# A linear recurrence taken two steps at a time, in SBUF, with the PSUM banks freed at the product

## The chip, the cores and the metric

The kernel runs on one core of one Trainium2 chip. The metric is the device time of one execution in microseconds (us).

## The reference, cut to what matters

A block of three layers on x (4 batches of 256 rows, 256 wide): cross-attention over 4,096 keys, a linear recurrence, and a mixture of experts. The change lies in the recurrence. For each batch and head it keeps a state of 16 ranks by 16 dimensions:

```python
def step(M, inp):
    q_t, k_t, v_t, g_t = inp
    M = M * decay + jnp.einsum('bhr,bhd->bhrd', g_t * k_t * scale, v_t)
    y = jnp.einsum('bhr,bhrd->bhd', q_t, M)
    return (M, y)
xs = (q_r.transpose(1, 0, 2, 3), k_r.transpose(1, 0, 2, 3), v.transpose(1, 0, 2, 3), g.transpose(1, 0, 2, 3))
M0 = jnp.zeros((b, h, r, d), dtype=x.dtype)
_, Y = jax.lax.scan(step, M0, xs)
```

Its output goes through a linear layer and a layer norm; then come a router that picks two of eight experts per row, the experts, and a shared feed-forward layer.

## The kernel before

Five engines run programs written out by hand and meet at semaphores: TensorE (PE), VectorE (DVE), ScalarE (ACT), GpSimd (POOL) and SyncE (SP), which issues the DMAs. Attention takes most of the time: 32 pairs of heads, each in 16 chunks. For each half chunk ACT makes the exponentials `PR`, and POOL adds them up in `acc` (L1803), for the row sums; after the last one it folds `acc` into `accf` (L1811).

The recurrence turns time into columns. A tile of 128 partitions holds 8 heads with 16 ranks each; the 512 columns are two batches of 256 time steps. With two halves of the heads and two pairs of batches there are four groups n, and in each 16 dimensions of the value, so 64 steps J = 16 n + s (`STEPS` is 16), each a whole recurrence over time for one dimension. A step is

- PE (L585, L586): the broadcast. Two matmuls spread one dimension of the value (`vh` and `vl`) over the ranks, into PSUM bank 4 or 5, by the parity of J.
- DVE (L1390): the product with the gated keys `kk`, in place in that bank.
- DVE (L1394): the scan over time, state = `dect` x state + product, out of `dect` (SBUF) and the bank (PSUM) into `M` (SBUF), which has two places.
- POOL (L1742): `qm` = `M` x queries `qr`, all in SBUF; eight places.
- PE (`sum_r`, L597): for every four steps the sum over ranks of four `qm`, issued within step 4q + 6, between that step's broadcast and the next.

`dect` is the decay, zero where a batch begins (from `seq`). The waits around a step: PE's broadcast of step J waits for the scan of step J - 2 (`m_done`), since the bank is free only then; DVE's product waits for the broadcast (`vb_ps`); the scan waits for the `qm` of step J - 2 (`qm_ready`), and POOL for the scan.

The order of the work around it is fixed by the program text. Steps 0 to 11 lie within the last three chunks of attention, two behind each half chunk; there POOL's `qm` stand between its sums of `acc`. Then come the last pair of heads' row sums, `copy_l`, `invert_l` and `divide`, the output projection and `add_rows` (L1320), with steps 12 to 15 between; the layer norm `norm_stats` and `norm_apply` (L1358); PE's transposes; and steps 18 to 47 with the projections of groups 2 and 3 between them (`lin_q`, `lin_k`, `lin_gate`, `lin_v`, `ranks` on PE, `rotate`, `keys`, `values_lo` on DVE), POOL's bias additions with steps 20 to 35 (L1749, L1751), and in group 2 the first half's output projection `mix_out` (L608), `add_out` (L1400), two more layer norms, `scale_rows` (L1405), the router (`below_max`, L1427, and `best_two`, from L1432) and the shared layer (`shared_product`, L1458). Steps 48 to 63 stand between the layers of the first experts (L653).

Of the kernel before, what the change touches and what calls it, by code (L numbers as in the profile page):

```python
# [27 lines left out]
def program(nc, nb, top, d, out):  # L28
# [4 lines left out]
    with ctx:  # L33
# [10 lines left out]
        def room(*tensors):  # L44
# [33 lines left out]
        we, = room(("we", [P, 3, 6, DM], F32))  # L78
        wel, gw, iota, sw12, sw3, be, hT, hTs, wT0, yacc0, t3, bc, zs, zT, lg, cand, sc2, hot, mx, sm, wm, wmT, *st_bc = room(
            ("wel", [P, 3, 6, DM], F32R), ("gw", [P, 2, E], F32), ("iota", [P, E], F32), ("sw12", [P, 2, 2, W], F32), ("sw3", [P, 4, DM], F32),  # L80
            ("be", [P, E, 3, 2], F32), ("hT", [P, 2, 2, W], F32), ("hTs", [P, 2, 2, W], F32R), ("wT0", [P, 2, W], F32),
            ("yacc0", [P, 2, W], F32), ("t3", [P, 2, 2, W], F32), ("bc", [P, 2, 2, W], F32), ("zs", [P, 2, W], F32), ("zT", [P, 4, W], F32),
            *[(x, [P, HR, E], F32) for x in ("lg", "cand", "sc2", "hot")], ("mx", [P, HR], F32), ("sm", [P, HR], F32),
            ("wm", [P, HR, 2 * E], F32), ("wmT", [2 * E, 2, W], F32), *norm_tiles("b"), *norm_tiles("c"))
        st_b, st_c = st_bc[0:3], st_bc[3:6]
# [159 lines left out]
        def _(sp):  # L245
# [190 lines left out]
        def _(pe):  # L436
# [139 lines left out]
            def step(J):  # L576
                n, s = J // STEPS, J % STEPS
                g, dd = n % 2, 4 * (s % 4) + s // 4
                if s == 0:
                    pe.wait_ge(vlo, n + 1)  # L580
                if J >= 2:
                    pe.wait_ge(m_done, J - 1)
                else:
                    pe.wait_ge([qr_ready, kk_ready][J], 2)
                pe.matmul(ps[:, 4 + J % 2, :], selvr[:, dd, :], vh[:, g, :], start=True, stop=False)  # L585
                pe.matmul(ps[:, 4 + J % 2, :], selvr[:, dd, :], vl[:, g, :], start=False, stop=True).then_inc(vb_ps, 1)  # L586
                if J >= 6 and J % 4 == 2:
# [671 lines left out]
        def _(dve):  # L1259
# [474 lines left out]
        def _(pool):  # L1734
            def step(J):
# [191 lines left out]
```

## Time and profile before

| | us |
|---|---|
| median of 3 runs | 2115.67 |
| lowest and highest run | 2111.74, 2115.80 |
| the profiled execution | 2115.32 |
| its span, first to last instruction | 2113.5 |
| PE busy in the span | 2016.6 (95%) |
| DVE busy | 1550.5 (73%) |
| POOL busy | 1434.4 (68%) |
| ACT busy | 1236.7 (59%) |

Busy shares are means over stages with different limits. The recurrence runs from 1757 to 1968 us of the span; what a change to it does is read from the rows of that stretch. Times in rows count from the span's start.

### The profile page before, as it was taken

The numbers are of one execution on the slowest core, as the hardware profiler recorded it, in microseconds if no ns is written. First come the engines' busy times: TensorE is split into PE (matmuls) and PEld (weight loads), VectorE is DVE, ScalarE is ACT, GpSimd is POOL, SyncE is SP. The second block draws the span as 40 slices with busy tenths as digits, with TensorE's granted clock in tenths as the row PEclk, the third lists the DMA queues.
The fourth block names the chain that finished last, engine by engine and source line by source line (L and its number), as shares of the span: only waits on it lengthen the run. The fifth ranks groups of instructions, "written<-read, shape, count | busy, mean of one in ns | idle before, by whom it ended". The sixth has DMA issues, their size and how long they took to land.

```text
span 2113.5 us, 47661 instructions
## 1 busy us (share of the span) xinstructions
PE 2016.6 (95%) x19694; PEld 1491.0 (71%) x19694; DVE 1550.5 (73%) x2004; ACT 1236.7 (59%) x1590; POOL 1434.4 (68%) x685
## 2 busy tenths in 40 slices
PE   5899999999999999999999999999999997779998
PEld 4677777777777777777777777777777743335466
DVE  5677777877777778777777787777777736887757
ACT  4566766676666676767666766676666662111333
POOL 3477777777777777777777777777777756633227
PEclk8999999999999999999999999999999998889999
DMA  8110101210101013101000130101010110203222
GB/s 219 29 27 14 29 14 34 74 29 14 29 14 29 15 33 75 28 18 25 23 20 25 23 87 16 29 14 29 14 29 4 47 39 1 76 29 97 76 60 71
DMA packets 45764, 82.15 MB, mean 39 GB/s; under 512 B 7120, under 2 KB 29008, under 8 KB 44912
## 3 DMA queue, kind: packets, MB, share of 16 engines
q1 hardware_dynamic: 45552, 79.10, 13.8%
q8 instruction: 160, 2.62, 0.5%
q14 instruction: 52, 0.43, 0.1%
HBM read 74.03 MB, written 5.05 MB: 37 GB/s over the span
## 4 chain that ended last, share of the span: by engine, by line
PE 79%; DVE 12%; issue 4%; POOL 2%; ACT 1%; DMA 1%; SPq 1%; POOLq 0%; DVEq 0%; ACTq 0%
PE ps L503 19%; PE ps L495 16%; PE ps L469 12%; PE ps L458 10%; PE ps L487 7%; PE ps L653 6%; DVE amx L1285 5%; DVE Otn L1307 2%; PE ps L449 1%; DVE V L1270 1%; PE ps L518 1%; DVE KL L1266 1%; PE ps L633 1%; POOL qm L1742 1%; PE ps L540 1%
## 5 line engine op out<-in xcount | busy, mean ns | idle before, releaser
L1803 POOL TENSOR_TENSOR acc<-acc,PR 128x1024 f32<-128x1024 f32 x480 | 1150.5, 2397 | 348.8 <-ACT PR L1156 310.1
L1285 DVE TENSOR_REDUCE amx<-ps 128x2 f32<-128x1024 f32 x512 | 623.9, 1219 | 195.9 <-PE ps L487 190.2
L1156 ACT ACTIVATE PR<-ps 128x1024 f32<-128x1024 f32 x512 | 518.8, 1019 | 208.9 <-PE ps L495 195.1
L503 PE MATMUL ps<-PR,V 128*64 128x256 f32 x4096 | 499.4, 386 | 0.4 <-ACT PR L1156 0.3
L503 PEld LDWEIGHTS ps<-PR,V 128*64 128x64 f32 x4096 | 271.2, 136 | 164.4 <-issue 27.2
L1006 ACT ACTIVATE ps<-NM 128x1024 f32<-128x1024 f32 x231 | 236.6, 1026 | 203.0 <-DVE V L1270 176.5
L469 PE MATMUL ps<-wv,C 64*128 64x256 f32 x4608 | 315.7, 281 | 1.2
L469 PEld LDWEIGHTS ps<-wv,C 64*128 64x128 f32 x4608 | 305.5, 187 | 11.9 <-issue 4.3
L458 PE MATMUL ps<-C,wk 64*128 64x512 f32 x2304 | 308.7, 395 | 5.3 <-DVE C L1262 4.2
L495 PE MATMUL ps<-qh,KH 64*128 64x256 f32 x2048 | 311.0, 297 | 0.8 <-ACT ps L1006 0.7
L495 PE MATMUL ps<-ql,KH 64*128 64x256 f32 x2048 | 293.4, 280 | 0.0
L495 PE MATMUL ps<-qh,KL 64*128 64x256 f32 x2048 | 293.1, 279 | 0.0
L495 PEld LDWEIGHTS ps<-qh,KH 64*128 64x128 f32 x2048 | 199.1, 186 | 76.1 <-issue 68.2
L458 PEld LDWEIGHTS ps<-C,wk 64*128 64x128 f32 x2304 | 221.5, 187 | 40.5 <-issue 8.6
L487 PE MATMUL ps<-KH,qh 64*128 64x512 f32 x1024 | 226.2, 437 | 23.0 <-DVE amx L1285 13.4
L1266 DVE TENSOR_TENSOR KL<-ps,KH 128x512 fp32r<-128x512 f32 x256 | 164.6, 685 | 61.9 <-ACT KH L997 59.5
L1567 DVE COPY ps<-NM 128x512 f32<-128x512 f32 x217 | 149.7, 690 | 76.1 <-ACT PR L1156 72.7
L495 PEld LDWEIGHTS ps<-ql,KH 64*128 64x128 f32 x2048 | 198.2, 187 | 5.6
L495 PEld LDWEIGHTS ps<-qh,KL 64*128 64x128 f32 x2048 | 198.1, 187 | 0.0
L997 ACT ACTIVATE KH<-ps 128x512 fp32r<-128x512 f32 x256 | 138.5, 593 | 90.0 <-PE ps L458 90.0
L1270 DVE COPY V<-ps 128x512 f32<-128x512 f32 x248 | 158.9, 682 | 19.7 <-PE ps L469 19.7
L487 PEld LDWEIGHTS ps<-KH,qh 64*128 64x128 f32 x1024 | 97.2, 186 | 92.0 <-issue 42.5
(198 smaller groups left out, 1900.2 us busy)
## 6 DMA issues: line engine op xcount, KB each, us to landing
wk<-wk_split SPq DMA_DIRECT2D x62, 192.0 KB, 3.4
wv<-wv_split SPq DMA_DIRECT2D x30, 384.0 KB, 4.8
bc<-wm_rows SPq DMA_DIRECT2D x32, 256.0 KB, 4.2
craw<-in_ctx SPq DMA_DIRECT2D x30, 256.0 KB, 4.2
we<-in_we SPq DMA_DIRECT2D x10, 768.0 KB, 4.4
wq<-in_wq SPq DMA_DIRECT2D x32, 128.0 KB, 2.9
wo<-in_wo SPq DMA_DIRECT2D x64, 64.0 KB, 2.2
craw<-in_ctx SPq DMA_DIRECT2D x30, 128.0 KB, 4.1
```

The lines of the kernel that those rows point to most:

```text
L458: mm = pe.matmul(out, wk[half(h), slot, 3 * w + t, :], C[half(h), 3 * c + t, j * CH:j * CH + CH], start=(i == 0), stop=(i == len(PARTS) - 1))
L469: mm = pe.matmul(out[:, k * 256:k * 256 + 256], C[half(h), 3 * c + t, keys], wv[half(h), 3 * w + t, :], start=(i == 0 and k == 0), stop=(i ...
L487: mm = pe.matmul(ps[:, 4 + h, :], qh[half(h), slot, t * P:t * P + P], KH[slot][half(h), c, :], start=True, stop=True)
L495: mm = pe.matmul(ps[:, first_bank + h, k * ROWS:k * ROWS + ROWS], keys_of[slot][half(h), c, keys], q[half(h), slot, :], start=False, stop= ...
L503: mm = pe.matmul(psO[half(h), :], V[:, c * KT + 2 * hf + k, hd * DH:hd * DH + DH], PR[:, slot, h, k, :], start=(first and hf == 0 and k == ...
L1006: act.activation(ps[:, first_bank:first_bank + 2, :].rearrange("p h (k n) -> p h k n", k=2), row.unsqueeze(2).to_broadcast([P, 2, 2, ROWS] ...
L1156: act.activation(PR[:, pr_slot(t, hf), :, :, :].rearrange("p h k n -> p (h k n)"), ps[:, bank:bank + 2, :].rearrange("p h n -> p (h n)"), ...
L1266: dve.tensor_tensor(KL[slot][:, c, :], bank, KH[slot][:, c, :].bitcast(F32), ALU.subtract).then_inc(k_lo, 1)
L1270: dve.tensor_copy(V[:, k:k + 2, :].rearrange("p a n -> p (a n)"), bank).then_inc(v_sb, 1)
L1285: dve.tensor_reduce(amx[:, :, t, c], psG, AX.X, ALU.max).then_inc(g_max, 1)
L1567: dve.tensor_copy(ps[:, score_bank(t, 1) + 1, :].rearrange("p (k n) -> p k n", k=2), NM[:, 1:2, :].to_broadcast([P, 2, ROWS])).then_inc(se ...
L1803: pool.tensor_tensor(flat(acc[:, :, :, :]), flat(acc[:, :, :, :]), flat(PR[:, pr_slot(t, hf), :, :, :]), ALU.add).then_inc(acc_done, 1)
```

## The change

Steps 0 to 47 are taken in pairs (J, J + 1). PE and POOL keep their instructions in their order. On DVE a pair is one product over both banks, 1,024 columns, that writes into two places of `M`, and one scan over the same 1,024 columns that reads `dect` and `M` and writes `M` in place. `M` has four places instead of two and `dect` holds every decay twice, side by side, so that one scan runs through two steps (the zero at the beginning of a batch cuts the state). Steps 48 to 63 have the same two instructions with 512 columns each. PE's broadcast waits for `kv_ready`, which the product raises, and no longer for `m_done` of the scan. The product waits for the `qm` of the pair before last. To make room, `seq` is loaded into the fourth place of `M`, and `ow` gets a place and a load later, behind `add_rows` of the last pair of heads.

```diff
-            ("t2", [P, 2, W], F32), ("gate", [P, W], F32), ("uT", [P, 2, 2, W], F32), ("dect", [P, 2, W], F32),
+            ("t2", [P, 2, W], F32), ("gate", [P, W], F32), ("uT", [P, 2, 2, W], F32), ("dect", [P, 2, 2, W], F32),
...
-            ("M", [P, 2, W], F32), ("qm", [P, 8, W], F32), ("selvr", [P, 16, P], F32R),
+            ("M", [P, 4, W], F32), ("qm", [P, 8, W], F32), ("selvr", [P, 16, P], F32R),
...
-        yT = uT
+        yT, seq = uT, M[:, 3, :]
...
-                sp.dma_start(ow[:], d["ow"]).then_inc(ow_in, 16)
...
             sp.wait_ge(x_added, PAIRS)
+            sp.dma_start(ow[:], d["ow"]).then_inc(ow_in, 16)
...
                 if J >= 2:
-                    pe.wait_ge(m_done, J - 1)
+                    pe.wait_ge(kv_ready, J - 1)
...
-            def step(J):
+            def steps(J, k):
+
                 n, s = J // STEPS, J % STEPS
-                g = n % 2
                 if s == 0:
                     dve.wait_ge(kk_ready, n + 1)
-                dve.wait_ge(vb_ps, J + 1)
-
-                bank = ps[:, 4 + J % 2, :]
-                dve.tensor_tensor(bank, bank, kk[:, g, :], ALU.mult).then_inc(kv_ready, 1)
-                dve.wait_ge(kv_ready, J + 1)
-                if J >= 2:
-                    dve.wait_ge(qm_ready, J - 1)
-                dve.tensor_tensor_scan(M[:, J % 2, :], dect[:, g, :], bank, 0.0, ALU.mult, ALU.add).then_inc(m_done, 1)
+                dve.wait_ge(vb_ps, J + k)
+                if J >= 4:
+                    dve.wait_ge(qm_ready, J + k - 4)
+                state = M[:, J % 4:J % 4 + k, :].rearrange("p a n -> p (a n)")
+                decay = dect[:, n % 2, 0:k, :].rearrange("p a n -> p (a n)")
+                dve.tensor_tensor(M[:, J % 4:J % 4 + k, :], ps[:, 4 + J % 2:4 + J % 2 + k, :],
+                                  kk[:, n % 2:n % 2 + 1, :].to_broadcast([P, k, W]), ALU.mult).then_inc(kv_ready, k)
+                dve.wait_ge(kv_ready, J + k)
+                dve.tensor_tensor_scan(state, decay, state, 0.0, ALU.mult, ALU.add).then_inc(m_done, k)
...
-                    for k in range(2 * EARLY):
-                        step(2 * EARLY * (t - 13) + k)
+                    for k in range(0, 2 * EARLY, 2):
+                        steps(2 * EARLY * (t - 13) + k, 2)
...
-            for J in range(6 * EARLY + 4, STEPS + 1):
-                step(J)
+            steps(STEPS, 2)
             norm_apply(na, 1, row, st_a)
             for n in range(3):
                 for s in range(STEPS):
-                    if STEPS * n + s <= STEPS:
+                    if STEPS * n + s <= STEPS + 1:
                         continue
-                    step(STEPS * n + s)
+                    if s % 2 == 0:
+                        steps(STEPS * n + s, 2)
```

On DVE, from the end of attention to the division of the last pair of heads; a row is line, operation, what it writes and reads, partitions by columns, and the semaphores it waits for (the scan is printed as SCALAR_TENSOR_TENSOR). Before:

```order
L1390 TENSOR_TENSOR ps<-ps,kk 128x512 [waits vb_ps]
L1394 SCALAR_TENSOR_TENSOR M<-dect,ps 128x512 [waits qm_ready,kv_ready]
L1299 COPY Ou<-ps 128x256 [waits ot_ready,pv_done]
L1320 TENSOR_TENSOR x<-ps,x 128x512 [waits x_added,out_ps]
L1390 TENSOR_TENSOR ps<-ps,kk 128x512 [waits vb_ps]
L1394 SCALAR_TENSOR_TENSOR M<-dect,ps 128x512 [waits qm_ready,kv_ready]
L1390 TENSOR_TENSOR ps<-ps,kk 128x512 [waits vb_ps]
L1394 SCALAR_TENSOR_TENSOR M<-dect,ps 128x512 [waits qm_ready,kv_ready]
L1303 COPY Otn<-ps 128x256 [waits l_ps]
L1307 RECIPROCAL Otn<-Otn 128x256 [waits l_sb]
L1313 TENSOR_TENSOR Otn<-Ou,Otn 128x256 [waits o_sb,rl_ready]
```

With the change:

```order
L1392 TENSOR_TENSOR M<-ps,kk 128x1024 [waits qm_ready,vb_ps]
L1395 SCALAR_TENSOR_TENSOR M<-dect,M 128x1024 [waits kv_ready]
L1299 COPY Ou<-ps 128x256 [waits ot_ready,pv_done]
L1320 TENSOR_TENSOR x<-ps,x 128x512 [waits x_added,out_ps]
L1392 TENSOR_TENSOR M<-ps,kk 128x1024 [waits qm_ready,vb_ps]
L1395 SCALAR_TENSOR_TENSOR M<-dect,M 128x1024 [waits kv_ready]
L1303 COPY Otn<-ps 128x256 [waits l_ps]
L1307 RECIPROCAL Otn<-Otn 128x256 [waits l_sb]
L1313 TENSOR_TENSOR Otn<-Ou,Otn 128x256 [waits o_sb,rl_ready]
L1392 TENSOR_TENSOR M<-ps,kk 128x1024 [waits qm_ready,vb_ps]
L1395 SCALAR_TENSOR_TENSOR M<-dect,M 128x1024 [waits kv_ready]
```

Two rows take the place of four, the product writes `M` and waits for `qm_ready`, the scan reads `M` in place of `ps` and waits for nothing but the product, and only one pair stands ahead of `copy_l`.

On DVE, ahead of the router's maximum (L1427, with the change L1428) in group 2. Before, with step 44 ahead of it and step 45 behind:

```order
L1390 TENSOR_TENSOR ps<-ps,kk 128x512 [waits vb_ps]
L1394 SCALAR_TENSOR_TENSOR M<-dect,ps 128x512 [waits qm_ready,kv_ready]
L1427 TENSOR_REDUCE mx<-ps 128x4 [waits lg_ps,g_in]
L1428 TENSOR_TENSOR lg<-ps,mx 128x32 [waits chain]
L1390 TENSOR_TENSOR ps<-ps,kk 128x512 [waits vb_ps,chain]
L1394 SCALAR_TENSOR_TENSOR M<-dect,ps 128x512 [waits qm_ready,kv_ready]
L1432 TENSOR_REDUCE sm<-lg 128x4 [waits ex]
```

With the change:

```order
L1392 TENSOR_TENSOR M<-ps,kk 128x1024 [waits qm_ready,vb_ps]
L1395 SCALAR_TENSOR_TENSOR M<-dect,M 128x1024 [waits kv_ready]
L1392 TENSOR_TENSOR M<-ps,kk 128x1024 [waits qm_ready,vb_ps]
L1395 SCALAR_TENSOR_TENSOR M<-dect,M 128x1024 [waits kv_ready]
L1428 TENSOR_REDUCE mx<-ps 128x4 [waits lg_ps,g_in]
L1429 TENSOR_TENSOR lg<-ps,mx 128x32 [waits chain]
L1433 TENSOR_REDUCE sm<-lg 128x4 [waits ex,chain]
```

Step 45 has moved ahead of the maximum, into the pair with step 44. In the same way step 17 has moved ahead of `norm_apply`, step 37 ahead of `add_out`, step 39 ahead of the `norm_apply` before the router and step 47 ahead of the shared products.

## Rows read from the trace of the kernel before

**Rows 1.** The page, its part on the chain that ended last: shares by engine.

```profile
PE 79%; DVE 12%; issue 4%; POOL 2%; ACT 1%; DMA 1%; SPq 1%; POOLq 0%; DVEq 0%; ACTq 0%
```

**Rows 2.** Busy time by stretch: length, each engine busy, PEclk, DMA share, GB/s.

```profile
1757.30:1785.40 28.10, 20.19 (x112) 10.38 (x112) 23.63 (x28) 6.33 (x6) 25.37 (x17) 0.88 0.00 1
1785.40:1804.70 19.30, 11.14 (x32) 5.12 (x33) 17.68 (x29) 1.52 (x5) 8.75 (x7) 0.52 0.35 118
1804.70:1854.90 50.20, 42.84 (x136) 19.83 (x136) 41.24 (x50) 6.22 (x8) 34.92 (x35) 0.88 0.08 34
1854.90:1907.30 52.40, 39.40 (x145) 20.08 (x145) 47.16 (x89) 9.06 (x17) 19.96 (x16) 0.87 0.15 51
1907.30:1968.00 60.70, 60.70 (x179) 28.85 (x177) 45.85 (x62) 6.79 (x10) 24.04 (x20) 1.00 0.30 87
```

**Rows 3.** Waits, 1757 to 1907 us: total, times, longest.

```profile
DVE ps L1390 <- PE ps L586: 12.9, 15, 2.7
```

**Rows 4.** Groups of DVE, shapes apart: count, busy us, mean ns, idle before.

```profile
L1285 DVE TENSOR_REDUCE amx<-ps 128x2 f32<-128x1024 f32 x512 | 623.9, 1219 | 195.9 <-PE ps L487 190.2
...
L1394 DVE TENSOR_TENSOR_SCAN M<-dect,ps 128x512 f32<-128x512 f32 x64 | 78.1, 1221 | 6.9 <-POOL qm L1742 4.8
...
L1390 DVE TENSOR_TENSOR ps<-ps,kk 128x512 f32<-128x512 f32 x64 | 44.1, 689 | 21.0 <-PE ps L586 20.9
...
L1703 DVE TENSOR_TENSOR wTs<-wT,wTs 128x1024 fp32r<-128x1024 f32 x1 | 1.2, 1215 | 0.0
```

**Rows 5.** Timeline of DVE, steps 20, 23, 26 and 35: start, duration.

```profile
1811.83 0.70 DVE L1390 TENSOR_TENSOR ps<-ps,kk 128x512 f32<-128x512 f32 x1 [0.90 <-PE ps L586]
...
1820.10 0.69 DVE L1390 TENSOR_TENSOR ps<-ps,kk 128x512 f32<-128x512 f32 x1
...
1825.65 0.68 DVE L1390 TENSOR_TENSOR ps<-ps,kk 128x512 f32<-128x512 f32 x1
...
1847.89 1.22 DVE L1394 TENSOR_TENSOR_SCAN M<-dect,ps 128x512 f32<-128x512 f32 x1
```

**Rows 6.** Timeline of POOL: `qm`, two `qm`, the fold of `acc`, a bias.

```profile
1759.44 1.27 POOL L1742 TENSOR_TENSOR qm<-M,qr 128x512 f32<-128x512 f32 x1 [10.78 <-DVE M L1394]
...
1764.79 2.50 POOL L1742 TENSOR_TENSOR qm<-M,qr 128x512 f32<-128x512 f32 x2
...
1784.08 1.27 POOL L1811 TENSOR_TENSOR accf<-acc 128x512 f32<-128x512 f32 x1
...
1825.28 0.73 POOL L1749 TENSOR_TENSOR u<-u,vecs 128x256 f32<-128x256 f32 x1
```

**Rows 7.** Timelines of DVE and POOL where both have two SBUF inputs.

```profile
391.23 2.37 POOL L1803 TENSOR_TENSOR acc<-acc,PR 128x1024 f32<-128x1024 f32 x1
392.50 2.71 DVE L1262 TENSOR_TENSOR C<-craw,C 128x1536 fp32r<-128x1536 f32 x1
393.74 3.72 POOL L1803 TENSOR_TENSOR acc<-acc,PR 128x1024 f32<-128x1024 f32 x1
...
1860.02 1.53 DVE L1405 SCALAR_TENSOR_TENSOR u<-u,mvb,vecs 128x256 f32<-128x256 f32 x1
...
2059.41 1.75 DVE L1498 TENSOR_TENSOR lox<-rawx,hix 128x1536 fp32r<-128x1536 f32 x1
2059.51 2.80 POOL L1766 TENSOR_TENSOR hTs<-hT,hTs 128x512 fp32r<-128x512 f32 x1 [2.58 <-ACT hTs L1066]
```

**Rows 8.** Timeline of PE: the sum over ranks at two clocks.

```profile
1805.85 1.94 PE L597 MATMUL ps<-qm,sely 128*32 128x512 f32 x8
...
1824.95 1.07 PE L597 MATMUL ps<-qm,sely 128*32 128x512 f32 x8
```

**Rows 9.** The second matmul of the broadcast: shortest, median and longest ns.

```profile
L586 PE MATMUL ps<-vl,selvr x64: 387/397/632, 1751.5 to 1964.2; 128*128 128x512 f32 x64
```

**Rows 10.** Timeline of DVE: step 45's product and the start of `best_two`.

```profile
1886.01 0.70 DVE L1390 TENSOR_TENSOR ps<-ps,kk 128x512 f32<-128x512 f32 x1 [1.71 <-PE ps L586]
...
1887.88 0.16 DVE L1432 TENSOR_REDUCE sm<-lg 128x4 f32<-128x32 f32 x1
```

More of the change, by code:

```diff
@@ L54, in program @@
         norm_tiles = lambda x: [("st6" + x, [P, NR, 6], F32), ("mv" + x, [P, NR, 2], F32), ("rs" + x, [P, NR], F32)]
-        (w4, bd, rope, t1, t2, gate, uT, dect, qr, kk, vh, vl, M, qm, selvr, ow, vecs, u, seq, sely, dl, dec, gb, *st_a) = room(
+        (w4, bd, rope, t1, t2, gate, uT, dect, qr, kk, vh, vl, M, qm, selvr, vecs, u, sely, dl, dec, gb, *st_a) = room(
             ("w4", [P, 4, 2, DM], F32), ("bd", [P, 2, 2, 2, P], F32), ("rope", [P, 2, W], F32), ("t1", [P, 2, W], F32),
-            ("t2", [P, 2, W], F32), ("gate", [P, W], F32), ("uT", [P, 2, 2, W], F32), ("dect", [P, 2, W], F32),
+            ("t2", [P, 2, W], F32), ("gate", [P, W], F32), ("uT", [P, 2, 2, W], F32), ("dect", [P, 2, 2, W], F32),
             ("qr", [P, 2, W], F32), ("kk", [P, 2, W], F32), ("vh", [P, 2, W], F32R), ("vl", [P, 2, W], F32R),
-            ("M", [P, 2, W], F32), ("qm", [P, 8, W], F32), ("selvr", [P, 16, P], F32R),
-            ("ow", [P, 2, DM], F32), ("vecs", [P, 3, DM], F32), ("u", [P, NR, DM], F32), ("seq", [P, W], F32),
+            ("M", [P, 4, W], F32), ("qm", [P, 8, W], F32), ("selvr", [P, 16, P], F32R),
+            ("vecs", [P, 3, DM], F32), ("u", [P, NR, DM], F32),
             ("sely", [P, 4, 32], F32), ("dl", [P, 2], F32), ("dec", [P, 2], F32), ("gb", [P, 2], F32), *norm_tiles("a"))
-        yT = uT
+        yT, seq = uT, M[:, 3, :]
         selv = qm[:, 0:4, :].rearrange("p a n -> p (a n)").rearrange("p (e c) -> p e c", e=16)
@@ L78, in program @@
         we, = room(("we", [P, 3, 6, DM], F32))
[L79 removed]
+        wel, gw, iota, sw12, sw3, be, hT, hTs, wT0, yacc0, t3, bc, zs, zT, lg, cand, sc2, hot, mx, sm, wm, wmT, ow, *st_bc = room(
             ("wel", [P, 3, 6, DM], F32R), ("gw", [P, 2, E], F32), ("iota", [P, E], F32), ("sw12", [P, 2, 2, W], F32), ("sw3", [P, 4, DM], F32),
@@ L83, in program @@
             *[(x, [P, HR, E], F32) for x in ("lg", "cand", "sc2", "hot")], ("mx", [P, HR], F32), ("sm", [P, HR], F32),
-            ("wm", [P, HR, 2 * E], F32), ("wmT", [2 * E, 2, W], F32), *norm_tiles("b"), *norm_tiles("c"))
+            ("wm", [P, HR, 2 * E], F32), ("wmT", [2 * E, 2, W], F32), ("ow", [P, 2, DM], F32), *norm_tiles("b"), *norm_tiles("c"))
         st_b, st_c = st_bc[0:3], st_bc[3:6]
@@ L328, in load_early @@
                 sp.dma_start(dl[:], d["dl"]).then_inc(r_in, 16)
-                sp.dma_start(seq[:], d["seq"][:, 0:W]).then_inc(r_in, 16)
+                sp.dma_start(seq, d["seq"][:, 0:W]).then_inc(r_in, 16)
                 sp.dma_start(bd[:], d["bd"]).then_inc(r_in, 16)
@@ L1515, in early @@
                     for g in range(2):
-                        dve.tensor_scalar(dect[:, g, :], seq[:, :], dec[:, g:g + 1], None, ALU.mult).then_inc(dect_ready, 1)
+                        dve.tensor_scalar(dect[:, g, :, :], seq.unsqueeze(1).to_broadcast([P, 2, W]), dec[:, g:g + 1], None, ALU.mult).then_inc(dect_ready, 1)
                     keys(0)
@@ L1620, in _ @@
             add_rows(nb - 1, PAIRS - 2, ps[:, 2, :])
-            step(6 * EARLY)
-            step(6 * EARLY + 1)
+            steps(6 * EARLY, 2)
             copy_l(PAIRS)
@@ L1625, in _ @@
             divide(PAIRS)
-            step(6 * EARLY + 2)
-            step(6 * EARLY + 3)
+            steps(6 * EARLY + 2, 2)
             add_rows(nb - 1, PAIRS - 1, ps[:, 0, :])
@@ L1666, in _ @@
             for s in range(4):
-                step(3 * STEPS + s)
+                steps(3 * STEPS + s, 1)
                 if s in (0, 1):
@@ L1673, in _ @@
                 weigh_third(X)
-                step(3 * STEPS + 4 + 3 * X)
+                steps(3 * STEPS + 4 + 3 * X, 1)
                 if X == 0:
@@ L1677, in _ @@
                 mask_third(X)
-                step(3 * STEPS + 5 + 3 * X)
+                steps(3 * STEPS + 5 + 3 * X, 1)
                 weigh_first(X + 1)
-                step(3 * STEPS + 6 + 3 * X)
+                steps(3 * STEPS + 6 + 3 * X, 1)
                 second_by_third(X)
@@ L1741, in step @@
                     pool.wait_ge(y_ps, J // 4 - 1)
-                pool.tensor_tensor(qm[:, J % 8, :], M[:, J % 2, :], qr[:, n % 2, :], ALU.mult).then_inc(qm_ready, 1)
+                pool.tensor_tensor(qm[:, J % 8, :], M[:, J % 4, :], qr[:, n % 2, :], ALU.mult).then_inc(qm_ready, 1)
             def biases(i):
```

## The prediction, on record before the changed kernel ran

> **What bounds the kernel now.** I read five views in turn. The chain of waits first: TensorE (PE) holds 79% of it, but PE's share is an average over the whole program [rows 1], and the change touches only the recurrence. So, second, the busy time by stretch [rows 2]. I cut the recurrence into A (end of attention), B (to the first broadcast behind the transposes), C (to `add_out`), D (to the first expert layer) and E (experts). PE fills E, 60.70 of 60.70 us. In A it is GpSimd (POOL) with 25.37 of 28.10 us, in B to D VectorE (DVE) is the busiest with 17.68 of 19.30, 41.24 of 50.20 and 47.16 of 52.40. A to D add up to 150 us, and what they lose moves everything behind them. Third, who waits for whom: DVE waits 12.9 us, in 15 places, for a broadcast [rows 3]. Fourth, what a step costs: product 689 ns, scan 1221 ns [rows 4]; undisturbed, three steps take 1825.65 - 1820.10 = 5.55 us, 1.85 each [rows 5]. Fifth, what DVE and POOL do to each other [rows 7], on which the sum turns.
>
> **The price of a pair on DVE.** The 1,024-column product reads PSUM as the chunk maximum does, 1219 ns for 1,024 columns; a subtraction from SBUF to SBUF takes 1215 [rows 4]: 1.22. The scan: a 512-column product and one of 1,536 (689 and 1750 ns [rows 4, 7]) give about 1.04 ns per column and 0.15 us fixed; the scan's 1221 ns is then 2 x 512 x 1.04 and the same fixed part, so 1,024 columns take 2.29. Back to back a step runs 0.06 us under its two durations, a pair then 3.45: 0.25 less than two steps, 6 us over 24 pairs. The bounds of a scan are 2.13 (no fixed part) and 2.44 (two scans); I take 2.29. The Trainium skill ("VectorE: DVE Perf Modes", the TRN2 errata) gives an operation out of SBUF 62 cycles less of fixed cost than one out of PSUM; by it, an estimate, 24 scans would save 1.6 us more. The two 1,024-column rows, 1215 and 1219 ns, show no such difference, and I take none.
>
> **The scan's second input.** Before, the scan read `dect` from SBUF and `ps` from PSUM; now both inputs are in SBUF. What such an operation does beside POOL is in [rows 7]. DVE's 1,536-column subtraction starts at 2059.41 and ends at 2061.16; POOL's product started at 2059.51 takes 2.80 instead of 1.27 [rows 6] and ends 1.15 after it: it stood still. The other way round, POOL's sum ran from 391.23 to 393.60; DVE's subtraction, begun at 392.50, took 2.71 instead of 1.75 and ended 1.61 after that sum; the next sum (393.74) then took 3.72. So one stands until the other is done, and a waiting one gets in between two of the other engine's. The scan of before overlaps `qm` without loss, having one input in SBUF. No row shows a scan with two. Bounds: nothing, or the full standstill; I take the full one, since three operations with two SBUF inputs (a product on POOL, a subtraction on DVE, and the 256 columns at 1860.02, which took 1.53, more than 1,024 columns elsewhere) all show it. The Trainium skill ("SBUF — State Buffer", Who interferes with whom) words this for every DVE instruction with two SBUF inputs beside a POOL instruction that reads SBUF: by it the sum is the one below, without it that of the first rival; for the scan no row of before decides.
>
> A scan that gets in between two POOL operations then lengthens POOL's chain by 2.29 - 0.15 + 1.15 - 1.24 = 2.05 us (1.24 is the spacing of two `qm` [rows 6]).
>
> **A.** POOL works without a gap to speak of from 1759.44 to `accf`'s end, 1784.08 + 1.27 = 1785.35 [rows 6]. Six scans (steps 2 to 13) now fall into this chain, the sixth before `accf` because DVE may run two pairs ahead: 6 x 2.05 = 12.3. The first `qm` starts 1.6 later (3.51 for a pair instead of 1.91), and 0.5 of idle time takes some of it. A: +13.4.
>
> **B.** `copy_l` used to wait behind steps 12 and 13 (-3.5). The division stands for one `qm` (+0.5); the pair 14, 15 must wait for step 15's broadcast, behind a row sum (+1.6); the pair 16, 17 stands whole ahead of `norm_apply` (+1.6), which now meets two `qm` instead of one (+1.05). B: +1.2.
>
> **C.** The first pair needs steps 18 and 19, with a row sum (1.94 us behind stretch B, whose granted clock of 0.52 is near the lower level of 1.2 GHz, 1.07 at the upper [rows 2, 8]) between them: +2.5. Then steps 20 to 35, where POOL has a `qm` (1.24) and a bias (0.7) per step. From the end of a scan, T: the product ends at T+1.2; the first `qm` (started T+0.14) lets go just then, the scan gets in and ends at T+3.5; the bias, then the second `qm`, end at T+4.0 and T+5.3. PE's row sum waits for that `qm`, and the pair's second broadcast stands behind it, two matmuls of 0.40 [rows 9]: T+6.3, T+6.9. Product to T+8.1; the scan finds the next pair's second `qm` running, waits to T+9.15 and ends at T+11.3. Four steps take 11.3 us instead of (1847.89 + 1.22 - 1811.83)/4 = 9.3 [rows 5]: +7.9 over sixteen. At the end `add_out` waits for steps 36 and 37: +1.3. C: +11.7.
>
> **D.** Step 37 no longer stands between the statistics and `scale_rows` (-1.85, -1.05 for the standstill at 1860.02, +0.35 for the root it hid); the pair 38, 39 stands ahead of `norm_apply` (+1.6, and +1.0 for a second `qm`); two steps as a pair (-0.25). `below_max` now waits for the pair 44, 45, whose second broadcast came at 1886.0: 1886.0 + 3.5, 0.9 for maximum and exponential, so `best_two` starts at 1890.4 by the old clock instead of 1887.88 [rows 10]: +2.5. The whole pair 46, 47 stands ahead of the shared products: +1.5. D: +3.8.
>
> **E and the small edits.** Steps 48 to 63 stay single; their scans too now have two SBUF inputs, but DVE has 15 us to spare against PE there [rows 2]: nothing. `dect`, twice as wide, is made before the recurrence, with DVE then idle for `vh`. `ow` loads from `add_rows` on, at the end of B; POOL's step 20 waits for it, several steps later, and SP's queue is one load longer, 70 us before the shared products need what follows. All at nothing.
>
> **Sum.** 13.4 + 1.2 + 11.7 + 3.8 = 30.1 us on the profiled execution's 2115.3 (span 2113.5; the median of the runs is 2115.67, 0.4 above): 2145.4, I say 2145.
>
> **The rivals.**
> *No standstill* (the scan does not share a path with POOL). Then A costs +1.1 (the first `qm`), B +0.6, C +2.8 (the paired broadcasts, less 0.25 a pair), D +3.8: +8.3, 2124. For it: no row has a scan with two SBUF inputs. Against: every other such operation stood. 12%.
> *Faster:* banks free at the product. A broadcast may start 2.3 us earlier, so that the 12.9 us for which DVE waits [rows 3] vanish, with 0.25 for each of the 18 pairs outside A: -17, 2098. It decides only if there is no standstill and both broadcasts of a pair, with the row sum or projection between them, end within a scan's 2.29 us. For it: between 1820.10 and 1825.65 DVE waits for no broadcast at all [rows 5]. Against: one row sum at the lower clock alone takes 1.94. 5%.
> *The change doesn't do what it says*, pairs being held by other waits so that gains and losses cancel: 2115. 3%.
> *More than I say:* POOL goes first each time (four steps in 12.4: +4.4) and PE runs at 1.2 GHz through C (row sum and broadcast 1.5 longer [rows 8, 9], four times: +6): 2156, the upper end of my own case.
>
> **How the numbers follow.** My case has 80%; its own range is 2130 to 2156. 2122 to 2156 takes in half of the first rival too and leaves out no more than 2 in 10. A change of 0.2%, 4 us, is about what a measurement of this kernel can tell from none. Slower: my case and the first rival, less what falls near zero: 0.90; same 0.05; faster 0.05.
>
> **What would show it.** The scan's row: 2.29 us where POOL is idle, and 3 us and more for many in A and C; `qm` with a maximum of about 3.5 us, never over 1.3 before. `accf` ends some 13 us later, `add_out` some 26, the first expert layer some 30; E keeps its 60.7. If scans stay at 2.29 and `qm` at 1.27 everywhere, the standstill was wrong; if A's POOL chain is no longer than before, the sum is.

## The result and the profile after

| | us |
|---|---|
| before, median of 4 runs beside those of the change | 2115.74 (2111.74 to 2118.18) |
| after, median of 4 runs | 2146.59 (2142.77 to 2149.57) |
| ratio, 95% interval | 1.0145, 1.0133 to 1.0157 |
| profiled execution of after; its span | 2146.78; 2145.0 |

The change costs 31 us, and all but 0.2 of it lies in A to D. Cut at the same events as before, the busy time by stretch of the kernel after (columns as in [rows 2]: length, PE, PEld, DVE, ACT, POOL, PEclk, DMA share, GB/s):

```profile
1757.30:1798.80 41.50, 24.07 (x112) 12.40 (x112) 28.06 (x17) 6.33 (x6) 37.10 (x17) 0.74 0.00 0
1798.80:1819.40 20.60, 9.65 (x33) 4.54 (x33) 15.56 (x22) 1.52 (x5) 10.11 (x9) 0.67 0.49 168
1819.40:1880.90 61.50, 47.47 (x148) 21.62 (x149) 43.51 (x30) 6.22 (x8) 43.26 (x34) 0.82 0.03 13
1880.90:1938.70 57.80, 37.25 (x134) 19.73 (x133) 44.65 (x77) 8.95 (x17) 19.72 (x16) 0.85 0.15 46
1938.70:1999.40 60.70, 60.70 (x181) 28.88 (x183) 47.30 (x62) 6.79 (x10) 24.09 (x20) 1.00 0.31 87
```

The reader should hold two columns of this against [rows 2]. E is 60.70 us again, with PE full. In A and C it is POOL that has more to do, 37.10 instead of 25.37 and 43.26 instead of 34.92 us, with the same number of instructions in A: some of them take longer. The groups of the kernel after, shapes apart (count, busy us and mean ns, idle before), say which:

```profile
L1395 DVE TENSOR_TENSOR_SCAN M<-dect,M 128x1024 f32<-128x1024 f32 x24 | 60.0, 2500 | 2.5
L1392 DVE TENSOR_TENSOR M<-ps,kk 128x1024 f32<-128x1024 f32 x24 | 29.3, 1220 | 39.9 <-PE ps L586 20.3 <-issue 13.5 <-POOL qm L1741 6.0
...
L1741 POOL TENSOR_TENSOR qm<-M,qr 128x512 f32<-128x512 f32 x64 | 90.8, 1430 | 115.9 <-DVE M L1395 106.2 <-issue 9.7
```

The paired product is what was forecast, 1.22 us. The paired scan has a mean of 2.50 where 2.29 was the price alone, and DVE idles 39.9 us ahead of the 24 products, 20.3 of them put down to a broadcast. The timeline of POOL in stretch A of the kernel after shows the mechanism:

```profile
1761.62 4.47 POOL L1741 TENSOR_TENSOR qm<-M,qr 128x512 f32<-128x512 f32 x2 [12.45 <-DVE M L1395]
1766.05 2.34 POOL L1802 TENSOR_TENSOR acc<-acc,PR 128x1024 f32<-128x1024 f32 x1
1768.35 4.49 POOL L1741 TENSOR_TENSOR qm<-M,qr 128x512 f32<-128x512 f32 x2
...
1775.13 2.54 POOL L1741 TENSOR_TENSOR qm<-M,qr 128x512 f32<-128x512 f32 x2
1777.62 4.34 POOL L1802 TENSOR_TENSOR acc<-acc,PR 128x1024 f32<-128x1024 f32 x1
1781.91 4.48 POOL L1741 TENSOR_TENSOR qm<-M,qr 128x512 f32<-128x512 f32 x2
...
1791.11 4.34 POOL L1802 TENSOR_TENSOR acc<-acc,PR 128x1024 f32<-128x1024 f32 x1
1795.53 3.27 POOL L1810 TENSOR_TENSOR accf<-acc 128x512 f32<-128x512 f32 x1
```

Two `qm` take 2.50 us [rows 6] and here 4.47, 4.49 and 4.48 in three cases; the sum into `acc` takes 2.37 [rows 7] and here 4.34 twice; `accf` 3.27 instead of 1.27. That is six times 1.97 to 2.00 us, 11.9 in all, where POOL stands while a scan gets in. In C three biases and two `qm` stand, and at other times the scans themselves; the timelines of DVE and POOL of the kernel after, around steps 22 to 25:

```profile
1834.21 1.23 DVE L1392 TENSOR_TENSOR M<-ps,kk 128x1024 f32<-128x1024 f32 x1 [0.69 <-issue]
1835.54 2.29 DVE L1395 TENSOR_TENSOR_SCAN M<-dect,M 128x1024 f32<-128x1024 f32 x1
...
1840.24 3.42 DVE L1395 TENSOR_TENSOR_SCAN M<-dect,M 128x1024 f32<-128x1024 f32 x1
```

```profile
1835.55 2.81 POOL L1750 TENSOR_TENSOR x<-x,vecs 128x256 f32<-128x256 f32 x1
...
1840.22 1.29 POOL L1741 TENSOR_TENSOR qm<-M,qr 128x512 f32<-128x512 f32 x1
1841.45 2.73 POOL L1750 TENSOR_TENSOR x<-x,vecs 128x256 f32<-128x256 f32 x1
```

A bias that starts 0.01 us after a scan takes 2.81 instead of 0.73 [rows 6]; a scan that starts 0.02 us after a `qm` takes 3.42 instead of 2.29. In both cases whoever came second stood.

### The profile page after: what moved, and what is told of

It is laid out like the page before. It is cut to its first block and busy times, and to the rows that moved or that the text cites. A ratio compares the mean times of both kernels' runs of the same rounds, so it can differ in the third digit from the quotient of the medians.

```text
span 2145.0 us, 47615 instructions
## 1 busy us (share of the span) xinstructions
PE 2021.8 (94%) x19694; PEld 1493.4 (70%) x19694; DVE 1554.1 (72%) x1956; ACT 1236.5 (58%) x1590; POOL 1455.8 (68%) x685
## 5 line engine op out<-in xcount | busy, mean ns | idle before, releaser
L469 PEld LDWEIGHTS ps<-wv,C 64*128 64x128 f32 x4608 | 305.5, 187 | 11.9 <-issue 4.3
L458 PEld LDWEIGHTS ps<-C,wk 64*128 64x128 f32 x2304 | 220.7, 187 | 40.9 <-issue 8.5
L1741 POOL TENSOR_TENSOR qm<-M,qr 128x512 f32<-128x512 f32 x64 | 90.8, 1430 | 115.9 <-DVE M L1395 106.2
```

The lines of the kernel that those rows point to most:

```text
L458: mm = pe.matmul(out, wk[half(h), slot, 3 * w + t, :], C[half(h), 3 * c + t, j * CH:j * CH + CH], start=(i == 0), stop=(i == len(PARTS) - 1))
L469: mm = pe.matmul(out[:, k * 256:k * 256 + 256], C[half(h), 3 * c + t, keys], wv[half(h), 3 * w + t, :], start=(i == 0 and k == 0), stop=(i ...
```

## The experiments

Eight kernels ran, each beside the kernel before on the same chip. For each one the stretches of its profiled execution were cut at the events of [rows 2]; A is counted from the start of `vl`'s step (1756.75 before), so that what the attention ahead of it varies by is left out. "16 steps" is from the product of step 20 to the end of the scan of step 35, a part of C. The table gives the lengths in us.

| kernel | median | ratio, 95% interval | A | B | C | 16 steps | D |
|---|---|---|---|---|---|---|---|
| before | | | 28.6 | 19.4 | 50.2 | 37.3 | 52.4 |
| after | 2146.59 | 1.0133 to 1.0157 | 41.5 | 20.6 | 61.5 | 44.5 | 57.8 |
| e1, POOL only writes in B to D | 2141.33 | 1.0108 to 1.0142 | 41.5 | 20.5 | 57.7 | 40.9 | 56.9 |
| e2, single steps into SBUF | 2130.88 | 1.006 to 1.0091 | 39.1 | 18.2 | 55.9 | 45.3 | 53.6 |
| e3, pairs out of the banks | 2162.97 | 1.0215 to 1.0246 | 34.9 | 23.9 | 76.7 | 58.1 | 61.6 |
| e4, only four places in `M` | 2113.47 | 0.998 to 0.9998 | 28.6 | 16.4 | 49.8 | 37.2 | 52.4 |
| e5, third group single | 2138.86 | 1.0102 to 1.0133 | 41.4 | 20.5 | 58.9 | 44.9 | 53.6 |
| e6, A single, out of the banks | 2134.15 | 1.008 to 1.011 | 28.6 | 19.0 | 62.3 | 44.5 | 59.8 |
| e7, PE's order in pairs too | 2142.32 | 1.0117 to 1.0145 | 41.4 | 20.4 | 59.7 | 42.0 | 54.3 |
| e8, e7 and POOL only writes | 2122.16 | 1.0021 to 1.0052 | 34.2 | 20.4 | 48.3 | 31.8 | 53.4 |

Before ran at a median of 2114.15 beside e1, e2, e3 and e6, at 2114.78 beside e4, e5 and e7, at 2116.72 beside e8.

The theory at the start: the scan of after has two SBUF inputs and excludes POOL's operations with two SBUF inputs (the *standstill*), and a pair waits for its second broadcast. The rivals: the standstill is not what costs, or pairing by itself costs nothing. In e1 and e8 POOL leaves out products and biases and only writes in their place, so these two measure time and nothing else.

**e1: POOL's reads taken away in B, C and D.**

```
-                pool.tensor_tensor(qm[:, J % 8, :], M[:, J % 4, :], qr[:, n % 2, :], ALU.mult).then_inc(qm_ready, 1)
+                if STEPS <= J < 3 * STEPS:
+                    pool.wait_ge(qm_ready, J)
+                    pool.memset(t3[:, :, :, :].rearrange("p a m n -> p (a m n)")[:, 0:1360], 0.0).then_inc(qm_ready, 1)
+                    return
+                pool.tensor_tensor(qm[:, J % 8, :], M[:, J % 4, :], qr[:, n % 2, :], ALU.mult).then_inc(qm_ready, 1)
```

The two biases became memsets of 688 columns in the same way.

> The changed kernel with POOL's qm of steps 16 to 47 and its biases replaced by memsets of about the same length (1,360 and 688 columns), which write SBUF and read nothing; the sums over ranks then add up old values and the biases are left out. Theory (a scan with two SBUF inputs and a POOL operation that reads SBUF stand still for one another): scans in stretches C and D take 2.29 to 2.35 us each, none above 2.5, the memsets keep their own length, steps 20 to 35 take 37 to 39 us instead of 44.5, and the time is 2135 to 2141. Rival (the cost is that of pairs: two broadcasts awaited, whole pairs ahead of the work behind): the time stays within 2 us of 2146.6. Stretch A is unchanged under both, its fold of acc ending 13 us later than in the kernel before.

Measured: 2141.33, just outside. The groups of e1 for the scan and the product (shapes apart, columns as above):

```profile
L1395 DVE TENSOR_TENSOR_SCAN M<-dect,M 128x1024 f32<-128x1024 f32 x24 | 57.3, 2387 | 2.5
L1392 DVE TENSOR_TENSOR M<-ps,kk 128x1024 f32<-128x1024 f32 x24 | 29.3, 1220 | 38.8 <-PE ps L586 22.2 <-issue 15.4 <-POOL qm L1745 1.2
```

The mean of the scan still holds the scans of A, up to 3.07 us. In C every scan takes 2.29 and every memset of 1,360 columns 1.23 us, also where the one starts 0.03 us behind the other; from the timeline of e1:

```profile
1851.07 2.29 DVE L1395 TENSOR_TENSOR_SCAN M<-dect,M 128x1024 f32<-128x1024 f32 x1
1851.10 1.23 POOL L1743 MEMSET t<- 128x1360 f32 x1
```

The standstill is gone there. But the 16 steps fall from 44.5 to 40.9 only, not to 37 to 39; the idle time ahead of the products stays at 38.8 us. So the standstill is real and its removal alone is worth little in C: DVE then waits for the broadcasts, and the 16 steps stay 3.6 us above before.

**e2: single steps in the old order, the product into SBUF.** The pairs go, the second SBUF input stays.

```
-                    for k in range(0, 2 * EARLY, 2):
-                        steps(2 * EARLY * (t - 13) + k, 2)
+                    for k in range(2 * EARLY):
+                        steps(2 * EARLY * (t - 13) + k, 1)
...
-                    if s % 2 == 0:
-                        steps(STEPS * n + s, 2)
+                    steps(STEPS * n + s, 1)
```

> Single steps in the order of the kernel before, but each product written into M and scanned there, with banks free at the product and four places in M. Theory (standstill): scans of 512 columns range from 1.22 to above 2.2 us, qm up to 2.4 us; twelve scans of 1.22 in stretch A's POOL chain cost 12 x (1.22 - 0.15 + 1.15 - 1.24) = 11.8 us, so that the fold of acc ends 11 to 13 us later than before; the time is 2130 to 2138. Rival (pairs): nothing of it is left, 2112 to 2117.

Measured: 2130.88, as the theory has it. A stays 10.5 us above before and C 5.7, while B is 1.1 below it and D 1.1 above. In the 16 steps single steps lose 8.0 us, more than the 7.2 of the pairs. Two rows of POOL in stretch A of e2, a sum and a double `qm`, show that single scans, too, let POOL stand:

```profile
1764.01 3.26 POOL L1804 TENSOR_TENSOR acc<-acc,PR 128x1024 f32<-128x1024 f32 x1
1767.24 4.35 POOL L1743 TENSOR_TENSOR qm<-M,qr 128x512 f32<-128x512 f32 x2
```

**e3: pairs, product and scan in the banks.** The second SBUF input goes, the pairs stay; the banks come free at the scan's end, as before the change.

```
-                    pe.wait_ge(kv_ready, J - 1)
+                    pe.wait_ge(m_done, J - 1)
...
-                state = M[:, J % 4:J % 4 + k, :].rearrange("p a n -> p (a n)")
-                dve.tensor_tensor(M[:, J % 4:J % 4 + k, :], ps[:, 4 + J % 2:4 + J % 2 + k, :],
-                                  kk[:, n % 2:n % 2 + 1, :].to_broadcast([P, k, W]), ALU.mult).then_inc(kv_ready, k)
+                bank = ps[:, 4 + J % 2:4 + J % 2 + k, :]
+                dve.tensor_tensor(bank, bank, kk[:, n % 2:n % 2 + 1, :].to_broadcast([P, k, W]), ALU.mult).then_inc(kv_ready, k)
...
-                dve.tensor_tensor_scan(state, decay, state, 0.0, ALU.mult, ALU.add).then_inc(m_done, k)
+                dve.tensor_tensor_scan(state, decay, bank.rearrange("p a n -> p (a n)"), 0.0, ALU.mult, ALU.add).then_inc(m_done, k)
```

> Pairs as in the change, but the product stays in its two banks and the scan of 1,024 columns reads them, so that the scan has one SBUF input and banks are free at its end. Theory (standstill): every scan takes 2.29 us and every qm at most 1.30; the fold of acc ends at most 4 us later than before. The time does not come back to that of before, since both broadcasts of a pair now follow the last scan: 2122 to 2140. Rival (pairs alone): 2145 or more, and the fold of acc as late as in the changed kernel, 13 us.

Measured: 2162.97, a clear miss, slower than after itself. What the theory said of the standstill holds: the scan's mean is 2287 ns and that of `qm` 1275, its longest 1.32 us. But A is 6.3 us longer than before, where at most 4 was expected. What the theory left out shows in the groups and in DVE's waits from 1757 to 1960 us of e3 (engine, awaited, total, times, longest):

```profile
L1395 DVE TENSOR_TENSOR_SCAN M<-dect,ps 128x1024 f32<-128x1024 f32 x24 | 54.9, 2287 | 2.2
L1741 POOL TENSOR_TENSOR qm<-M,qr 128x512 f32<-128x512 f32 x64 | 81.0, 1275 | 153.1 <-DVE M L1395 141.1 <-issue 12.0
...
DVE ps L1391 <- PE ps L586: 65.7, 21, 7.3
```

and in one pair's round, all engines of e3 in order of time:

```profile
1830.64 2.29 DVE L1395 TENSOR_TENSOR_SCAN M<-dect,ps 128x1024 f32<-128x1024 f32 x1
...
1832.98 0.50 PE L585 MATMUL ps<-vh,selvr 128*128 128x512 f32 x1 [3.77 <-DVE M L1395]
...
1833.72 1.94 PE L597 MATMUL ps<-qm,sely 128*32 128x512 f32 x8
...
1838.28 0.40 PE L586 MATMUL ps<-vl,selvr 128*128 128x512 f32 x1
1838.78 1.23 DVE L1391 TENSOR_TENSOR ps<-ps,kk 128x1024 f32<-128x1024 f32 x1 [4.68 <-PE ps L586]
```

Both banks are held until the scan ends (1832.93); only then does PE write the first, sum the rows, multiply a projection and write the second. In this round PE does nothing while DVE scans, and the pair takes 9.5 us (7.3 is the mean over the 16 steps). Neither e1 nor e3 has the standstill in C; they differ there above all in when the banks come free, and the 16 steps take 40.9 and 58.1 us. So it is the early release that makes pairs bearable.

**e6: after, with the 16 steps of A single and out of the banks.** In A the body of `steps` does as before; the broadcasts there wait for `m_done`.

```
+                if J < STEPS:
+                    for j in range(J, J + k):
+                        bank = ps[:, 4 + j % 2, :]
+                        dve.tensor_tensor(bank, bank, kk[:, n % 2, :], ALU.mult).then_inc(kv_ready, 1)
...
+                        dve.tensor_tensor_scan(M[:, j % 4, :], dect[:, n % 2, 0, :], bank, 0.0, ALU.mult, ALU.add).then_inc(m_done, 1)
+                    return
```

> The changed kernel with steps 0 to 15 single and scanned out of PSUM, as before; pairs in SBUF from step 16 on. Theory (standstill): stretch A loses nothing but a place or two in the order, the fold of acc ends within 2 us of the kernel before, and the time is 2131 to 2136. Rival (in A only the later first qm of a pair counts, 1.6 us): 2144 to 2146.

Measured: 2134.15. A is 28.6 us, that of before to 0.1, and the time falls by 12.4: what A loses is lost to the whole kernel. D is 2.1 us longer than in after. 2.0 of these lie behind the start of `best_two`, where the granted clock is 0.93 instead of 1.00 and DVE waits 3.59 us instead of 2.11 for the broadcast of step 48; why the clock was lower there is open. As e6 takes the pairs out of A too, it does not by itself tell them from the second input; e2, which has single steps with that input, does.

**e4: of the change only the four places of `M`.** The wider `dect` and the later load of `ow` stay as well. Single steps, product and scan in the bank, banks released at the scan's end; the scan waits for the row product of four steps back and not of two. Against the kernel before:

```
-                if J >= 2:
-                    dve.wait_ge(qm_ready, J - 1)
-                dve.tensor_tensor_scan(M[:, J % 2, :], dect[:, g, :], bank, 0.0, ALU.mult, ALU.add).then_inc(m_done, 1)
+                if J >= 4:
+                    dve.wait_ge(qm_ready, J + k - 4)
+                dve.tensor_tensor_scan(state, decay, bank.rearrange("p a n -> p (a n)"), 0.0, ALU.mult, ALU.add).then_inc(m_done, k)
```

> Single steps with product and scan out of the bank, as before; of the change only four places in M are kept. Theory (the product into SBUF, and with it the scan's second SBUF input, is what costs single steps 15 us): the wait of a scan for the row product two steps back goes, POOL sets A as before (accf ends within 0.5 us of before), the copy of the sums in B need not stand behind steps 12 and 13 (-3), and C and D do not move, since DVE waits there for broadcasts that still start at the end of a scan: 2112, between 2109 and 2115. Scans 1.22 and row products 1.27 us throughout. Rival (the places themselves, the wider decay, the moved load or the order cost something): above 2118.

Measured: 2113.47, ratio 0.9989 (0.998 to 0.9998): a gain at the edge of what can be told, and none of the rival's cost. B is 3.0 us shorter. A row of DVE in B of the kernel before, the scan of step 12, and the same scan in e4:

```profile
1786.68 1.22 DVE L1394 TENSOR_TENSOR_SCAN M<-dect,ps 128x512 f32<-128x512 f32 x1 [1.52 <-POOL qm L1742]
```

```profile
1784.61 1.22 DVE L1395 TENSOR_TENSOR_SCAN M<-dect,ps 128x512 f32<-128x512 f32 x1
```

The 1.52 us for `qm` are gone. e2 and e4 have the same steps in the same order; they differ in where the product goes and when the bank comes free, and in 17 us. The bank comes free earlier in e2, the slower one, so what costs there is the product in SBUF.

**e5: after, with steps 32 to 47 single.**

```
-                    if s % 2 == 0:
+                    if n == 2:
+                        steps(STEPS * n + s, 1)
+                    elif s % 2 == 0:
```

> The changed kernel with its third group (steps 32 to 47) in single steps in the old order, product still into SBUF. Theory (in D the pairs cost because the softmax's maximum, the routing and the shared products wait for a pair's second broadcast): D falls back from +5.3 to about +1, C loses the 1.5 us that add_out waits for steps 36 and 37: 2141, between 2138 and 2143. Rival (D's 5.3 us are the standstill and the lower clock, not the pairs): 2145 to 2148.

Measured: 2138.86, inside the theory's range. D is 53.6, 1.2 above before, and C loses 2.6 of its length in after, where 1.5 was expected. So 4.1 of D's 5.3 us are the pairs.

**e7: PE's order in pairs too.** From step 16 to 47 the two broadcasts of a pair stand together; row sum, projections, transposes and logits come behind the second.

```
-                if J >= 6 and J % 4 == 2:
+                if J >= 6 and J % 4 == (3 if STEPS < J < 3 * STEPS else 2):
...
-                    step(STEPS * n + s)
+                    if s % 2 == 0:
+                        step(STEPS * n + s)
+                        step(STEPS * n + s + 1)
```

> The changed kernel with PE's order from step 16 to 47 in pairs too: the two broadcasts of a pair stand next to each other, row sum, projections, transposes and logits behind the second. Theory (outside the standstill the loss of C and D is the pair's second broadcast, which stands behind such work): DVE's waits for broadcasts shrink, C loses 3 to 6 of its 11.3 us more than before, D 1 to 3, A stays: 2139, between 2135 and 2143. Rival 1 (the standstill sets C, the broadcasts only fill its gaps): 2145 to 2149. Rival 2 (what is put behind, the projections and the routing, is now late itself): above 2149.

Measured: 2142.32, at the slow end of the theory's range, and its split was off. D gains 3.5, C only 1.8: the 16 steps gain 2.5 and the first pair 1.9, but from step 35's scan to `add_out` it takes 10.2 us instead of 7.7, since `mix_out`, ahead of the pair 36, 37, now starts 2.0 us after that scan has ended and not 0.8 us before: the row sum that it needs is now behind a broadcast more. That part is rival 2's. In steps 28 to 35 the pairs follow one another every 5.80 us, about what POOL needs for two `qm`, two biases and a scan that gets in (2 x 1.24 + 2 x 0.7 + 1.97 = 5.85): with PE's order mended, POOL is the bound.

**e8: e7, and POOL without SBUF reads in A too.** The edits of e1 and e7, and in A:

```
+                if J < STEPS:
+                    pool.memset(qm[:, J % 8, :], 0.0).then_inc(pz, 1)
+                    pool.wait_ge(pz, J + 1)
+                    pool.memset(qm[:, J % 8, :], 0.0).then_inc(qm_ready, 1)
+                    return
```

> Both together, and in A too: PE's broadcasts in pairs as in the run before, and POOL, in place of the row products of steps 0 to 47 and of the biases, only writes (two memsets of 512 columns per step in A, one of 1,360 per step and one of 688 per bias behind it), so that the row sums add other values and the biases are left out. Theory (standstill and PE's order are two losses that add up): A +1 to +3 instead of +13, steps 20 to 35 in 44.5 - 3.6 - 2.5 = 38.4 us, C +4 to +7, D +1 to +3: 2124, between 2120 and 2128. Rival 1 (without the standstill, paired broadcasts let the pairs run back to back: 8 x 3.45 and 7 other operations of 0.68, 33 to 35 us): C below that of before, 2112 to 2118. Rival 2 (A's 13 us are not POOL's reads but the pair itself): A stays at +10 or more, 2133 or above.

Measured: 2122.16, in the theory's range, yet by other parts. The 16 steps take 31.8 us: not 38.4, and less than rival 1's 33 to 35, so rival 1 had the mechanism, though not the time (2112 to 2118), since A stayed longer. The timeline of DVE in e8 from step 24 on:

```profile
1827.98 1.21 DVE L1395 TENSOR_TENSOR M<-ps,kk 128x1024 f32<-128x1024 f32 x1
1829.29 2.29 DVE L1398 TENSOR_TENSOR_SCAN M<-dect,M 128x1024 f32<-128x1024 f32 x1
1831.50 1.20 DVE L1395 TENSOR_TENSOR M<-ps,kk 128x1024 f32<-128x1024 f32 x1
1832.81 2.29 DVE L1398 TENSOR_TENSOR_SCAN M<-dect,M 128x1024 f32<-128x1024 f32 x1
1835.01 0.67 DVE L1382 SCALAR_TENSOR_TENSOR kk<-ps,gate 128x512 f32<-128x512 f32 x1
```

No wait is left between them, a pair every 3.52 us. Each of the two losses alone hides the other: taking away the standstill alone gained 3.6 us in these steps, the broadcasts' order alone 2.5, both together 12.7. A was 5.6 us above before, not 1 to 3: the sums of `acc` and `accf` still read SBUF, and three of them stood, as POOL's timeline of e8 in A shows:

```profile
1762.70 3.41 POOL L1816 TENSOR_TENSOR acc<-acc,PR 128x1024 f32<-128x1024 f32 x1
...
1779.29 3.48 POOL L1816 TENSOR_TENSOR acc<-acc,PR 128x1024 f32<-128x1024 f32 x1
...
1787.26 3.16 POOL L1824 TENSOR_TENSOR accf<-acc 128x512 f32<-128x512 f32 x1
```

Against 2.37 and 1.27 these are 1.0, 1.1 and 1.9 us, 4.0 of the 5.6. This A is no clean measure, since two memsets take about 1.05 us of POOL's chain where a `qm` takes 1.24.

## Why the prediction was right

The forecast was 2145 us and the time is 2146.59. By its steps:

| step | forecast | measured |
|---|---|---|
| A | +13.4 | +13.4, of which 0.5 is the attention ahead |
| B | +1.2 | +1.2 |
| C | +11.7 | +11.3 |
| of it, 16 steps | +7.9 | +7.2 |
| D | +3.8 | +5.3 |
| E and all behind it | 0 | +0.2 |
| sum | +30.1 | +31.5 by the spans |

**The price of a pair.** 1.22 and 2.29 us were read from other operations' rows and both came true: 1220 ns, and 2287 in e3, where nothing disturbs the scan. Back to back a pair takes 3.52 us and not 3.45 (e8), so it saves 0.18 us against two steps and not 0.25.

**A.** The agreement to 0.1 us is luck in part: 0.5 of the 13.4 belongs to the attention ahead, and A itself costs 12.9. The six scans came to 11.9 where 12.3 was forecast, the late first `qm` to 1.7 where 1.6 was, and the idle time gave back the 0.5.

**The scan's second input.** The step on which the sum turned, taken at full size with no row of before to decide it, was right: six scans in POOL's chain at 1.97 to 2.00 us each, where 2.05 was forecast; `qm` has a maximum of 3.26 us, a little below the 3.5. e6 and e4 show that A's part goes when the second input goes, and e2 that it stays when only the pairs go. The Trainium skill ("SBUF — State Buffer", Who interferes with whom) goes further than the forecast did: the contention is with a POOL instruction that reads SBUF, not with one that only writes it. The traces of e1 and e8 agree: a scan beside nothing but memsets, of 0.52 and 1.23 us, keeps its 2.29.

**B.** The sum is right, but two of its five terms are off and cancel. By the timelines of DVE before and after, the copy gains 3.1 us and not 3.5, and the division, which was to lose 0.5, loses 0.1. The pair 14, 15 costs 1.7, the pair 16, 17 1.8 and `norm_apply` 0.8, where 1.6, 1.6 and 1.05 were forecast. e4 confirms the first: with the wait for `qm` gone, the copy comes early and B is 3.0 us shorter.

**C.** The size of the 16 steps was right to 0.7 us. The round of the forecast, in which scan, `qm`, row sum and the second broadcast follow one another, exists, but not as a steady round of 11.3 us per four steps: they take 10.2, 11.1, 15.4 and 7.9 us, so that the close sum is luck in part. The round shows plainest behind the scan of steps 28 and 29 of the kernel after (1851.30 to 1854.06), in its timelines of POOL, PE and DVE:

```profile
1851.87 3.25 POOL L1741 TENSOR_TENSOR qm<-M,qr 128x512 f32<-128x512 f32 x1
```

```profile
1855.17 1.93 PE L597 MATMUL ps<-qm,sely 128*32 128x512 f32 x8 [2.70 <-POOL qm L1741]
```

```profile
1858.35 1.23 DVE L1392 TENSOR_TENSOR M<-ps,kk 128x1024 f32<-128x1024 f32 x1 [3.71 <-PE ps L586]
```

The `qm` stands beside the scan, the row sum waits for the `qm`, and the product waits for the broadcast behind the row sum. It is a chain of both causes, which fits that e1 and e7, each of which takes out one link, gain little. The first pair came to 2.2 where 2.5 was forecast, the tail to 1.9 where 1.3 was.

**D, the term that was mis-sized.** Forecast +3.8, measured +5.3. From `add_out` to the keys of the last group it is +0.3 and not -0.2; from there to `best_two` +3.3 and not +2.5; the shared products +1.7 and not +1.5. The step on `below_max` started from the broadcast of step 45 at its old distance behind the keys, but before the keys are done PE cannot start the transposes, and behind those stand the broadcasts of 42 and 43 with a row sum between them. Before, DVE had step 41 to do between the keys and the broadcast of 42; in pairs it has only `values_lo`. The row of DVE for step 42 of the kernel before:

```profile
1877.79 0.70 DVE L1390 TENSOR_TENSOR ps<-ps,kk 128x512 f32<-128x512 f32 x1 [0.49 <-PE ps L586]
```

The timelines of PE and DVE of the kernel after:

```profile
1901.32 1.94 PE L532 MATMUL ps<-ident_sb,u 128*128 128x128 f32 x8 [7.88 <-DVE kk L1379]
...
1904.04 1.94 PE L597 MATMUL ps<-qm,sely 128*32 128x512 f32 x8
1905.91 0.80 PE L585 MATMUL ps<-vh,selvr 128*128 128x512 f32 x1
1906.50 0.50 PE L586 MATMUL ps<-vl,selvr 128*128 128x512 f32 x1
```

```profile
1907.10 1.22 DVE L1392 TENSOR_TENSOR M<-ps,kk 128x1024 f32<-128x1024 f32 x1 [5.28 <-issue]
...
1913.24 1.22 DVE L1392 TENSOR_TENSOR M<-ps,kk 128x1024 f32<-128x1024 f32 x1 [2.52 <-PE ps L586]
```

DVE waits 5.28 us for the pair 42, 43, where it had waited 0.49, after PE has itself waited 7.88 for the keys. The row sum takes 1.94 us, as at the lower clock of [rows 8]. e5 takes the pairs away and D falls to +1.2; e7 moves the row sum behind the second broadcast and D falls to +1.9.

**The rivals.** *No standstill*, 2124: e8 comes closest to trying it and gives 2122, but with PE's order changed as well and the sums of A still standing. Its price of C was too low: +2.8, where e1, without the standstill in C, has +7.5. The forecast thus gave the standstill 8.9 us of C by itself; taking it away gives back 3.8 (e1 against after), or 11.4 where the broadcasts are paired already (e8 against e7). *Faster*, 2098: its two conditions were the right ones. With both met in B to D of e8, the 16 steps take 31.8 us instead of 37.3 and C is 1.9 us shorter than before; A, B and D keep it from paying over the whole kernel. *The change doesn't do what it says*: the groups show 24 pairs.

## What to carry to other kernels

Before an intermediate is moved from PSUM to SBUF to free a bank, count the SBUF inputs of the operation that reads it next: with two of them on DVE, a POOL operation that reads SBUF stands while that operation runs, and the reverse. A chain on POOL that was the bound then grew by nearly the whole operation, 2.0 us for each scan of 2.29 here. When work is issued in larger units, give the engine that feeds it the same units, or the second feed of each stands behind whatever lay between the two; but look at what then moves behind it, as at the end of C in e7. And when two losses fill the same gap, take both away in one run before either is called small: 3.6 and 2.5 us apart were 12.7 together.

## What the runs showed of the hardware that was not expected

The standstill has no fixed loser; how finely the start decides was not expected. In the kernel after, the timelines of C shown above have now the bias longer (2.81 us for 0.73) and now the scan (3.42 for 2.29), by which of the two began 0.01 or 0.02 us earlier.

The granted clock of PE, whose two levels are 1.2 and 2.4 GHz, was on average another in each form of the 16 steps. From busy time by stretch, the kernel after, e3 and e8 (columns as above):

```profile
1828.72:1873.24 44.52, 30.59 (x92) 12.98 (x93) 33.97 (x23) 3.97 (x6) 36.37 (x28) 0.81 0.00 1
```

```profile
1829.32:1887.38 58.06, 34.23 (x91) 14.34 (x92) 31.68 (x23) 3.83 (x6) 27.11 (x28) 0.79 0.00 0
```

```profile
1818.56:1850.34 31.78, 27.34 (x92) 11.52 (x90) 30.96 (x23) 2.68 (x5) 25.79 (x29) 0.95 0.00 1
```

PE's 91 or 92 recorded matmuls are busy 27.3 us at a mean granted clock of 0.95 in e8, and 34.2 at 0.79 in e3. In the round of C shown above PE waits 2.70 us for a `qm`, and the row sum behind it takes 1.93 us, as at the lower level in [rows 8]. Broadcasts and row sums thus come later in their turn where the clock is low. How much of the loss of after is this was not measured apart, and no run here shows what sets the clock.
